# Decayed keys and queries by GpSimd; the first norm's sum kept in PSUM and its tokens written from there, in another place

## The reference, cut to what matters

```
tok:  each 4x4 window of pixels is averaged to one token (256 tokens per map); the token's layer-normed
      value is the query, the 16 layer-normed pixels are keys and values of 8 heads
      h = mean + softmax(q k / 8) v @ proj_w.T + proj_b
attn: causal attention with decay in chunks of 128 tokens (two chunks per map, 8 heads, D = 8)
      scores = (qi @ ki.T) * mask ;  intra = scores @ vi
      inter  = (qi * q_dec) @ S   ;  S_new = blk * S + (ki * k_dec).T @ vi ;  S = 0 before chunk 0
      out    = (intra + inter) @ w_proj + b_proj
h = layernorm(h + attn(h))
ffn:  8 experts, top 2, weighted by softmax, gelu ;  h = layernorm(h + ffn(h))
```

## Time and profile before

| | |
|---|---|
| median of 3 runs | 2586.48 us (2584.95 to 2589.83) |
| profiled execution | 2589.41 us, span 2587.0 us |
| mean granted TensorE clock | 0.985 |
| busy in the span | PE 87%, DVE 79%, ACT 72%, POOL 71% |
| first stage | to about 2165 us |
| second stage | the rest |

### The profile page before, as it was taken

The page is one execution under the profiler, slowest core; times in us unless marked ns, Lnnn a source line. Parts: engine busy times, 40 slices in busy tenths (PEclk is TensorE's granted clock), DMA queues, the critical chain, the costliest instruction groups (busy, mean ns, idle before and its releaser), DMA issues. The chain is left out here.

```text
span 2587.0 us, 91002 instructions
## 1 busy us (share of the span) xinstructions
PE 2248.5 (87%) x32685; PEld 1057.8 (41%) x32685; DVE 2053.0 (79%) x3996; ACT 1851.1 (72%) x4405; POOL 1839.2 (71%) x1949
## 2 busy tenths in 40 slices
PE   1888898888888888888888888888888885999997
PEld 1344444444444444444444444444444442222222
DVE  4588888887888888888888888888888886777775
ACT  2877777777777777777777777777777773555554
POOL 3688788887888888888888888888888862233333
PEclk9999999999999999999999999999999996999999
DMA  4433333333333333333333333333333300010001
GB/s 79 83 67 67 66 66 66 67 66 57 64 67 67 67 67 67 67 67 67 67 67 67 67 67 67 67 67 67 67 67 67 67 2 1 17 23 22 20 20 29
DMA packets 573783, 147.92 MB, mean 57 GB/s; under 512 B 573504, under 2 KB 573504, under 8 KB 573504
## 3 DMA queue, kind: packets, MB, share of 16 engines
q1 hardware_dynamic: 573504, 143.53, 29.0%
HBM read 135.10 MB, written 8.39 MB: 55 GB/s over the span
## 5 line engine op out<-in xcount | busy, mean ns | idle before, releaser
L709 POOL TENSOR_TENSOR pv<-vs,aw 128x512 f32<-128x512 f32 x512 | 540.2, 1086 | 306.5 <-DVE aw L912 306.5
L856 DVE TENSOR_TENSOR kqs<-ps,qqT 128x512 f32<-128x512 f32 x512 | 354.1, 692 | 299.5 <-PE ps L393 295.2
L595 ACT ACTIVATE xd<-xb 128x512 f32<-128x512 f32 x512 | 585.4, 1178 | 0.0
L388 PE MATMUL ps<-xb,w_ckv 64*64 64x512 f32 x2048 | 555.6, 619 | 5.0 <-DVE kqs L856 5.0
L393 PE MATMUL ps<-xb,w_ckv 64*64 64x512 f32 x2048 | 555.6, 619 | 0.0
L577 ACT ACTIVATE sqs<-ps 128x512 f32<-128x512 f32 x512 | 308.4, 602 | 247.2 <-PE ps L393 246.9
L753 POOL TENSOR_TENSOR xt<-xb 128x512 f32<-128x512 f32 x256 | 325.8, 1273 | 23.0 <-issue 22.6
L716 POOL TENSOR_TENSOR pv<-pv 128x512 f32<-128x512 f32 x256 | 320.5, 1271 | 0.0
L867 DVE TENSOR_TENSOR sm<-ps,decay 128x1024 f32<-128x1024 f32 x256 | 299.5, 1208 | 4.4 <-PE ps L471 4.4
L415 PE MATMUL ps<-w_ckv,xd 64*64 64x64 f32 x16384 | 301.1, 223 | 0.0
L415 PEld LDWEIGHTS ps<-w_ckv,xd 64*64 64x64 f32 x16384 | 266.1, 136 | 33.1 <-issue 3.0
(11 more groups left out here) (223 smaller groups left out, 4261.6 us busy)
## 6 DMA issues: line engine op xcount, KB each, us to landing
xb<-in_x_dram SPq DMA_DIRECT2D x512, 256.0 KB, 4.4
out_dram<-outb SPq DMA_DIRECT2D x128, 64.0 KB, 1.6
w1p<-in_L_ffn_w_dram SPq DMA_DIRECT2D x16, 16.0 KB
w2p<-in_L_ffn_w_dram SPq DMA_DIRECT2D x8, 16.0 KB
b1p<-in_L_ffn_b_dram SPq DMA_DIRECT2D x8, 0.2 KB
b2v<-in_L_ffn_b_dram SPq DMA_DIRECT2D x8, 2.0 KB
sm<-in_L_tok_Wkv_dram SPq DMA_DIRECT2D x4, 16.0 KB, 2.0
w_av<-in_L_attn_w_qkv_dram SPq DMA_DIRECT2D x4, 16.0 KB, 2.1
```

The costliest lines, as they stand in the source:

```text
L388: nc.tensor.matmul(KB[own, :], w_ckv[own, 2 * P + m * C:2 * P + (m + 1) * C], xv[own, j], start=True, stop=True)
L595: nc.scalar.activation(xd[:, j, :].rearrange("p (b t) -> p b t", b=ST), xb[:, f, :].rearrange("p (b t d) -> p d b t", b=ST, d=ST)[:, j], A ...
L709: nc.gpsimd.tensor_tensor(pv[:, at].rearrange("p (k d) -> p k d", d=D), vs[:, s, at].rearrange("p (k d) -> p k d", d=D), aw[:, j * W4:(j + ...
L856: V.tensor_tensor(kqs[:, j, :].rearrange("p (t d) -> p t d", d=ST), KB.rearrange("p (t d) -> p t d", d=ST), qqT[:, s, :].unsqueeze(2).to_b ...
```

## The change

`kd` and `qdm` are made by GpSimd instead of VectorE, behind `htok`. The sum `lt` isn't an SBUF tensor any more: VectorE adds `htok` to the projection in place, in columns 128 to 271 of PSUM bank 5 (`LT`), and ScalarE's squares read it there. The normalised tokens (`h1` of unit u-5) are written by one instruction for both halves, from PSUM, and in another place: behind `q2` instead of behind `hT`, with a wait for `oT_done`. `sblk` and `lt` change places. TensorE's `attend(0)` waits for the squares (`ln_sq`) instead of `lt_done`, and `attended` waits for `h1_done`.

```diff
@@ -96,6 +96,7 @@
         QB = [ps[:, g, :] for g in range(4)]
         SB = ps[:, 4, :]
         B5 = ps[:, 5, :]
+        LT = B5[:, P:P + 2 * CR]
         B6 = ps[:, 6, :]
         B7 = ps[:, 7, :]
         B67 = ps[:, 6:8, :]
@@ -195,7 +196,6 @@
             htok = sb1("htok", [P, 2, 2 * CR])
             qm = sb1("qm", [P, 2, 4 * P])
             oT = sb1("oT", [P, P])
-            lt = sb1("lt", [P, 2 * CR])
 
             ld_w = sem("ld_w")
             s_zero = sem("s_zero")
@@ -477,7 +477,7 @@
                             keys_free(part + 1)
                             return
                         if part == 0:
-                            pe.wait_ge(lt_done, done(i, r, 5, 1))
+                            pe.wait_ge(ln_sq, done(i, r, 5, 1))
                             pe.wait_ge(vk_ev, done(i, r, 4, 2))
                             pe.wait_ge(mask_done, done(i, r, 4, NM))
                             if s == 1:
@@ -515,7 +515,8 @@
 
                         if there(i, r, 4):
                             pe.wait_ge(oT_done, done(i, r, 4, 1))
-                            nc.tensor.matmul(B5[:, P:P + 2 * CR], oT[:], w_ap[:], start=True, stop=True).then_inc(pr_done, 1)
+                            pe.wait_ge(h1_done, done(i, r, 5, 1))
+                            nc.tensor.matmul(LT, oT[:], w_ap[:], start=True, stop=True).then_inc(pr_done, 1)
 
                     def state():
 
@@ -616,7 +617,7 @@
 
                         act.wait_ge(lt_done, done(i, r, 5, 1))
                         for m in range(2):
-                            ins = squares(lt[:, m * CR:m * CR + C], ssq[:, m:m + 1], l2[:, m * C:(m + 1) * C])
+                            ins = squares(LT[:, m * CR:m * CR + C], ssq[:, m:m + 1], l2[:, m * C:(m + 1) * C])
                         ins.then_inc(ln_sq, 1)
                     if there(i, r, 3):
                         act.wait_ge(vk_pe, done(i, r, 3, 1))
@@ -728,6 +729,16 @@
                         pool.wait_ge(vk_ev, done(i, r, 3, 2))
                         nc.gpsimd.tensor_tensor(htok[:, o, :], htok[:, o, :], bp_row[:],
                                                 ALU.add).then_inc(hb_done, 1)
+                        if s == 1:
+                            pool.wait_ge(st_ev, pairs(i, r, 0, 2))
+                            pool.wait_ge(s_pe, pairs(i, r, -1))
+                            nc.gpsimd.tensor_tensor(kd[:].rearrange("p (m h d) -> p m h d", m=2, d=D),
+                                                    kpl[:].rearrange("p (m h d) -> p m h d", m=2, d=D),
+                                                    kdec[:].unsqueeze(1).unsqueeze(3).to_broadcast([P, 2, HEADS, D]),
+                                                    ALU.mult).then_inc(kd_done, 1)
+                        else:
+                            pool.wait_ge(o_done, done(i, r, 5, 1))
+                            nc.gpsimd.tensor_tensor(qdm[:], qT[:, o, :], qdec[:], ALU.mult).then_inc(qd_done, 1)
 
                     def normalised():
 
@@ -890,6 +901,11 @@
                         dve.wait_ge(tq_pe, done(i, r, 0, 1))
                         V.tensor_tensor(heads(q2[:]), B67[:, :, 0:C], yrs[:, 2:4, 2:3].to_broadcast([P, 2, C]),
                                         ALU.mult).then_inc(q2_done, 1)
+                    if there(i, r, 5):
+                        dve.wait_ge(oT_done, done(i, r, 4, 1))
+                        V.tensor_tensor(h1[:, bass.ds(4 * i + r - 5, 1), :].rearrange("p o (m c) -> p (o m) c", c=CR),
+                                        LT.rearrange("p (m c) -> p m c", c=CR),
+                                        yrs[:, 0:2, 2:3].to_broadcast([P, 2, CR]), ALU.mult).then_inc(h1_done, 1)
                     keys(2)
                     link, n = chain(dve, soft_ch, done(i, r, 2, 5))
                     rs_b = yrs[:, :, 0:2].unsqueeze(3).to_broadcast([P, N, 2, HEADS])
@@ -924,36 +940,17 @@
                         V.scalar_tensor_tensor(hT[:, s, :].unsqueeze(1), B6[:, P:2 * P].unsqueeze(1), pb_col[:, 0:1],
                                                h1[:, bass.ds(4 * i + r - 2, 1), 0:P],
                                                ALU.add, ALU.add).then_inc(hT_done, 1)
-                    if there(i, r, 5):
-                        for m in range(2):
-                            ins = V.tensor_scalar(h1[:, bass.ds(4 * i + r - 5, 1), m * CR:(m + 1) * CR],
-                                                  lt[:, m * CR:(m + 1) * CR].unsqueeze(1), yrs[:, m, 2:3], None, ALU.mult)
-                        ins.then_inc(h1_done, 1)
-                    if there(i, r, 3) and s == 1:
-                        dve.wait_ge(st_ev, pairs(i, r, 0, 2))
-                        dve.wait_ge(s_pe, pairs(i, r, -1))
-                        V.tensor_tensor(kd[:].rearrange("p (m h d) -> p m h d", m=2, d=D),
-                                        kpl[:].rearrange("p (m h d) -> p m h d", m=2, d=D),
-                                        kdec[:].unsqueeze(1).unsqueeze(3).to_broadcast([P, 2, HEADS, D]),
-                                        ALU.mult).then_inc(kd_done, 1)
-                    if there(i, r, 3) and s == 0:
-                        dve.wait_ge(o_done, done(i, r, 5, 1))
-                        dve.wait_ge(qk_ev, done(i, r, 3, 2))
-                        V.tensor_tensor(qdm[:], qT[:, o, :], qdec[:], ALU.mult).then_inc(qd_done, 1)
                     if there(i, r, 4):
                         dve.wait_ge(pr_done, done(i, r, 4, 1))
-                        dve.wait_ge(h1_done, done(i, r, 5, 1))
                         dve.wait_ge(hb_done, done(i, r, 4, 1))
-                        dve.wait_ge(ln_sq, done(i, r, 5, 1))
                         if s == 0:
                             dve.wait_ge(s_pe, pairs(i, r, -1))
-                        V.tensor_tensor(lt[:], B5[:, P:P + 2 * CR], htok[:, s, :], ALU.add).then_inc(lt_done, 1)
-                        if s == 0:
                             dve.wait_ge(o_done, done(i, r, 5, 1))
                             V.tensor_tensor(sblk[:].rearrange("p (j d) -> p j d", d=D),
                                             B5[:, 3 * P:4 * P].rearrange("p (j d) -> p j d", d=D),
                                             headmask[:].unsqueeze(2).to_broadcast([P, SL, D]),
                                             ALU.mult).then_inc(sb_done, 1)
+                        V.tensor_tensor(LT, LT, htok[:, s, :], ALU.add).then_inc(lt_done, 1)
                 units(dve, step)
```

## The result

The changed kernel takes 2467.05 us (median of 4 runs, 2463.1 to 2468.09), against 2585.72 us before (4 runs). The ratio is 0.9537, 95% interval 0.9525 to 0.9548. The forecast was 2458 us (2435 to 2512), and faster. The profiled execution took 2467.41 us, its span is 2465.5 us against 2587.0 us.

What follows compares the result with a forecast made beforehand. The prediction took a ring of waits, not one engine, as the bound: 16.24 us a step. Saving 1.04 us in 123.6 steps gives 128.5 us, so 2589.41 becomes 2461, median 2458 us (range 2435 to 2512).

Steps and rivals of the forecast that it cites:

- (a): VectorE between `hT` and `lt`: `kd` or `qdm` leaves, one per step, 1.21 us (1.14 start to start).
- (b): VectorE between `hT` and `lt`: the two `h1` writes leave, 1.29 us.
- (c): TensorE at `attn_vk`: `kT` is late next, so about 1.17 us a step goes, giving 15.07 us a step.
- (d): GpSimd's path from `aw` through `pv`, `agg` and `kqs(1)` to the next `aw`: 15.30 us a step, 0.94 less.
- (e): Start of the stage, nearly this case in the earlier trace: 15.09 us; 15.2 taken, 1.04 us a step gained.
- (f): GpSimd behind `htok`: `kd` or `qdm` adds 0.42 us (0.28 to 1.2), with 0.7 us to spare at `aggn`.
- (g): VectorE behind `q2`: the added `h1` write takes 0.30 us, has 0.2 us cover, costs 0, at most 0.5.
- (h): ScalarE's squares reading PSUM, and the new waits of `attend(0)` and `attended` on TensorE: cost 0.
- B: Rival, chance 0.18: the moved `h1` write on VectorE is late, 0.5 us exposed each step; 2520 us, half exposed 2489.
- C: Rival, chance 0.13: GpSimd's chain shortens without VectorE competing, TensorE's path bounds; 2442 us, or 2430 with earlier `kT`.
- D: Rival, chance 0.05: no change, the wait comes back elsewhere, such as at ScalarE's `kT`; 2586 us.
- E: Rival, chance 0.04: slower, the moved `h1` write waits for ports GpSimd holds and takes 1.70 us; 2605 us.

## Why the prediction was right, point by point

(a), (b) The removal. Right in size between `hT` and `lt`. Wrong in how I split it: the 1.14 and 1.29 us are not the prices of two edits. The runs with one part each gave 0.9688 and 0.9527 against 0.9537 for both, so moving `kd` and `qdm` added nothing to the other part. Once the two `h1` writes are gone, `kd` costs VectorE 0.38 us and not 1.21. The change's effect came by the `h1` write, which became one instruction and left its place; the merging alone, in the old place, gave 0.9641, three quarters of it. The GpSimd move alone would have brought two thirds.

The start of the first mask was 0.6 us off: I let it begin when two of the four scores were done, half way through TensorE's group. It starts 1.20 us after the group starts (1208.47 to 1209.67), at its end. The first mask ended at about 1210.9 and `kT` at 1211.09, later still, so it cost nothing.

(c) TensorE's next wait is `kT`, as forecast, but it was sized too small: 0.47 us in the step shown, where the forecast left 0.27 (1219.25 to 1219.52). I had let `attn_vk` start 0.07 us after the end of `kT`'s eviction; it starts 0.25 us after it (1211.09 to 1211.34), the median of all 118 steps too. With that TensorE's path comes to about 15.25 us instead of 15.07, level with the 15.30 of GpSimd's.

(d), (e) GpSimd's path. From `aw` to `kqs(1)` I had 9.43 us and the step shown has 9.33 (1206.61 to 1215.94). In it `agg` waits for `pv`. In the next step `kqs(1)`, at 1230.99, waits 0.19 us for TensorE, so the two paths take turns; the runs with more work on GpSimd and with an early `kT` show both. I had taken 15.2 us a step, between the pair of the earlier trace rows and my own sum of 15.30; 15.22 was measured. That value was a choice between two numbers, and in part luck: I had taken the two paths to be 0.23 us apart, and they were nearly level.

The step gained 1.07 us for 1.04, yet the first stage was 123 us shorter and not 128.5: the 123.6 steps were too many. The ninth `aw` started only 2.1 us earlier than before (203.5 to 201.4), so the first eight steps gained little. The last one started 125.6 us earlier (2135.2 to 2009.6), and the end of the stage behind it takes 2.7 us more (33.9 to 36.6). These 5.7 us, the second stage's 1.3, and the 2.9 us that I took off for the profiled execution, which lies only 0.4 us over the median now, are to half a microsecond the 9 us between forecast and measurement.

(f) `kd` and `qdm` on GpSimd take 0.408 and 0.462 us in the median, for 0.42 taken. The doubled load (the unused product behind them) cost nothing. GpSimd's idle time ahead of the products is 1.28 us and not 0.9: its wait ahead of `aggn`, 31.1 us in all before, is 0.5 now.

(g) The `h1` write takes 0.306 to 0.310 us in all 128 cases, for 0.30. I gave it 0.2 us of cover; in the step shown it has 0.10 after its end, and no cost can be seen. The real cover is larger: a write of 1.00 us in the same place, with `lt` in SBUF, cost nothing either.

(h) As forecast: neither `attend(0)` nor `attended` has a wait for these in the list.

Rivals. B: the write does wait for `oT` (33.0 us in 116 steps), but behind the wait it was hidden. C: the other path did not become the only one. D: TensorE waited for `kT`, for 56.1 / 118 = 0.48 us, where it had waited 1.44 for the mask. E: with `lt` in SBUF the write did reach 1.05 us and was not slower in all. Its point of decision, 1.55 us, was counted from the start of `kqs(2)`, where I should have counted from the work that needs it; the rival was weaker than written.

## What to carry to other kernels

Instructions of VectorE that contend with GpSimd should not stand in a row while GpSimd runs back to back. The first waits for what is left of GpSimd's instruction, which may be little or all of it; each further one begins just as the next one does, and pays the whole of it. Merge them, or scatter them, before moving work to the other engine: the one-instruction edit (ratio 0.9641) brought more than the move to GpSimd (0.9688). And when a stall goes, list what ends second at that wait and on each ring that passes it, as the shorter of these gains is what remains.

## What the runs showed of the hardware

A contended `kd` isn't a fixed 1.21 us: with the same operands it was 0.28 us (GpSimd idle), 0.38 in the median behind one PSUM instruction, 1.16 behind one contending instruction and 1.21 behind two. The Trainium skill, "SBUF — State Buffer", section "Who interferes with whom", says that whoever issues first gets the shared ports for its whole instruction. The runs agree, and they add what happens in a row: the loser gets its turn, and then loses again to the next instruction. What decides is the moment: beside products of 1.08 us, a contending instruction that started 0.80 us or more behind the product's start took 0.25 to 0.45 us, and one that started 0.01 to 0.03 us behind it 1.11 to 1.21. It goes the other way too: in the run with `kd` and `qdm` back on VectorE, 27 of the 119 started within 0.01 us of a product's start and took 0.28 us, and GpSimd's product beside them took 1.22 to 1.23 us.

The four scores of 32 rows each are issued as one group of 1.14 us, and the first mask, which needs only two of them, starts when the whole group ends. In the trace of the changed kernel each score is two passes, and the second passes of all four end within 0.02 us of each other (the profile models these ends), which fits with a mask that starts no sooner for two of them than for all.
